# The opening part of a graph and mixture layer on one core: x normalised first, on two engines, with the edge tables behind it

## What is computed

```python
xn = _layernorm(x, axis=-1)                         # (x - mean) / sqrt(var + 1e-5)
x = x + gnn(xn, edges) + mix(xn)
x = x + ffn(_layernorm(x, axis=-1))
# gnn: msg_sum = segment_sum(xn[src], dst); mean = msg_sum / max(count, 1); two linear maps, relu, a third map
# mix: linear attention: kv = k^T v over all nodes, then q kv, gelu, w2
# ffn: a shared expert plus the best 2 of 8 experts for each row
```

## Time and profile before

| | us |
|---|---|
| median of 3 runs | 2733.04 (2730.94 to 2736.2) |
| profiled execution, own time | 2729.84 |
| its span | 2728.1 |
| its mean granted TensorE clock | 0.947 of full |
| busy PE, POOL, DVE, ACT | 2360.3, 1854.2, 1072.0, 801.6 |

### The profile page before, as it was taken

The page is one execution under the profiler, slowest core; times in us unless marked ns, Lnnn a source line. Parts: engine busy times, 40 slices in busy tenths (PEclk is TensorE's granted clock), DMA queues, the critical chain, the costliest instruction groups (busy, mean ns, idle before and its releaser), DMA issues.

```text
span 2728.1 us, 51754 instructions
## 1 busy us (share of the span) xinstructions
PE 2360.3 (87%) x12344; PEld 2030.3 (74%) x12345; DVE 1072.0 (39%) x3479; ACT 801.6 (29%) x1897; POOL 1854.2 (68%) x1790
## 2 busy tenths in 40 slices
PE   0688867877789999999999999999999999997998
PEld 0455556666678888888788888888887888876987
DVE  8545443333333343333343343433333333432221
ACT  1234312222223323232323233232323233223332
POOL 2677767777777777777777777777777777751221
PEclk9899978888899999999999999999999999998999
DMA  8333433344355555555555555555555555544764
GB/s 276 84 104 101 120 92 113 107 115 115 113 159 161 175 145 172 144 175 153 166 163 148 171 143 172 143 174 142 175 155 162 164 146 175 143 143 125 225 182 108
DMA packets 256254, 405.91 MB, mean 149 GB/s; under 512 B 70073, under 2 KB 187001, under 8 KB 255578
## 3 DMA queue, kind: packets, MB, share of 16 engines
q0 software_dynamic: 95360, 232.54, 31.9%
q1 hardware_dynamic: 154218, 164.36, 18.6%
q10 hardware_dynamic: 6384, 6.42, 0.7%
HBM read 362.16 MB, written 41.01 MB: 148 GB/s over the span
## 4 chain that ended last, share of the span: by engine, by line
PE 57%; issue 14%; POOL 13%; DVE 7%; DMA 4%; DVEq 2%; ACT 1%; ACTq 1%; POOLq 0%; SPq 0%; PEldq 0%
PE p_agg L1400 15%; POOL region L521 13%; PE p_h L1610 10%; PE p_y L1621 10%; PE p_h L1578 5%; PE p_h L1736 3%; PE p_a L1610 2%; PE p_y L1584 2%; DMA region<-xn_d,idx_s 2%; PE p_agg L1762 2%; PE p_a L1552 1%; PE p_c L1561 1%; PE p_a L1550 1%; PE p_y L1762 1%; PE p_t L1429 1%
## 5 line engine op out<-in xcount | busy, mean ns | idle before, releaser
L521 POOL DMA_INDIRECT region<-xn_d,idx_s x1568 | 1555.4, 992 | 573.3 <-issue 467.0
L1400 PE MATMUL p_agg<-region,onehot 128*128 128x258 f32 x3136 | 781.5, 403 | 123.2 <-DMA region<-xn_d,idx_s 106.4
L1400 PEld LDWEIGHTS p_agg<-region,onehot 128*128 128x128 f32 x3136 | 619.0, 201 | 234.0 <-issue 116.1
L1610 PE MATMUL p_h<-wkv_s,region 128*128 128x256 f32 x936 | 277.3, 458 | 105.8 <-ACT wkv_s L670 105.8
L1610 PEld LDWEIGHTS p_h<-wkv_s,region 128*128 128x128 f32 x936 | 210.3, 231 | 157.9 <-issue 120.7
L868 DVE TENSOR_TENSOR late<-late,p_agg 128x258 f32 x176 | 74.6, 424 | 612.3 <-PE p_agg L1400 438.4
L862 DVE TENSOR_TENSOR onehot<-row_s,iota_s 128x896 f32<-128x896 f32 (+1 forms) x225 | 246.0, 1093 | 172.4 <-issue 169.5
L1621 PE MATMUL p_y<-region 128*128 128x256 f32 x1248 | 282.3, 379 | 0.0
L691 ACT ACTIVATE work<-p_h,b1s_s 128x128 f32<-128x128 f32 x392 | 112.0, 368 | 511.6 <-PE p_h L1578 511.6
L1621 PEld LDWEIGHTS p_y<-region 128*128 128x128 f32 x1248 | 236.9, 190 | 32.5
L1584 PE MATMUL p_y<-w2s_s,work 128*128 128x256 f32 x768 | 197.3, 379 | 0.0
(11 more groups left out here) (256 smaller groups left out, 2900.3 us busy)
## 6 DMA issues: line engine op xcount, KB each, us to landing
region<-in_w1p SPq DMA_DIRECT2D x55, 1024.0 KB
region<-in_w2p SPq DMA_DIRECT2D x55, 1024.0 KB, 10.0
region<-xn_d,idx_s POOLq DMA_INDIRECT x1568
rows_s<-slot_d SPq DMA_DIRECT2D x39, 258.0 KB
region<-in_x SPq DMA_DIRECT2D x7, 896.0 KB, 5.1
xn_d<-region ACTq DMA_DIRECT2D x7, 896.0 KB, 7.0
rows<-in_x SPq DMA_DIRECT2D x49, 128.0 KB, 2.3
xnr_s<-xn_d SPq DMA_DIRECT2D x49, 128.0 KB, 2.7
```

The source lines that it names most:

```text
L521: pool.indirect_dma_start(out=ring[b][:, u, 0:D], out_offset=None, in_=xn_d, in_offset=IND(ap=idx_s[b][:, u:u + 1], axis=0)).then_inc(s_ro ...
L1400: m = mm(p_agg[b % 2], onehot[:, b % 2, u, :], ring[b][:, u, :], start=u == 0, stop=u == U - 1)
L1610: m = mm(h_wide[j], w1p_s[0][:, c, j * P:(j + 1) * P], xgt_s[:, c, :], start=c == 0, stop=c == KD - 1)
```

## The change

Four edits to the opening part:

- SP loads x first and `dst` behind the seventh chunk. The first four loads of indices stand ahead of the wait for `xnst`.
- VectorE runs the loop over the chunks first, and the work on `dst` behind it.
- In each chunk ScalarE normalises 5 of the 7 tiles (`BY_ACT = 5`), as x times scale plus bias, from rs and a new column nb = -mean times rs that VectorE writes. VectorE keeps 2 tiles. ScalarE waits for both parts before it stores the chunk.
- TensorE raises `pass_` by 4 before its waits.

```diff
+BY_ACT = 5
@@ sync
-            sp.dma_start(dst32_s, dst).then_inc(S["dstin"], 16)
             for c in range(NT // XCH):
                 if c:
                     sp.wait_ge(S["xin"], 16 * c)
                 sp.dma_start(x_s[:, c * XCH:(c + 1) * XCH, :],
...
+            sp.dma_start(dst32_s, dst).then_inc(S["dstin"], 16)
             for to, of in loads:
                 sp.dma_start(to, of).then_inc(S["wts"], 16)
 
             sp.wait_ge(S["const"], 3)
             sp.dma_start(out[NP:NP + P // 2, :], zero_s[0:P // 2, :]).then_inc(S["ost"], 16)
-            sp.wait_ge(S["xnst"], 16 * (NT // XCH))
...
             for b in range(RING):
                 load_idx(b, NI - 1)
+            sp.wait_ge(S["xnst"], 16 * (NT // XCH))
             sp.wait_ge(S["span"], 2)
@@ scalar, in the loop over the chunks
                 nc.scalar.activation(sd_s[:, 0:XCH], ve_s[:, 0:XCH], ACT.Sqrt).then_inc(S["sd"], 1)
+                act.wait_ge(S["nrm"], c + 1)
+                for j in range(BY_ACT):
+                    xj = x_s[:, ds(c * XCH + j, 1), :].squeeze(1)
+                    i = nc.scalar.activation(xj, xj, ACT.Identity, bias=nb_s[:, j:j + 1], scale=rs_s[:, j:j + 1])
+                i.then_inc(S["xna"], 1)
+                act.wait_ge(S["xna"], c + 1)
                 act.wait_ge(S["xn"], c + 1)
@@ vector
-            dve.wait_ge(S["dstin"], 16)
-            def pads_first(to):
-                V.tensor_copy(to[:, 0:2 * U], dst32_s[:, NG * U:])
-                return V.tensor_copy(to[:, 2 * U:], dst32_s[:, 0:NG * U])
-
-            own.step(pads_first(dst_s))
-            own.step(V.tensor_scalar(dst32_s, dst32_s, P - 1, None, ALU.bitwise_and))
-            own.step(pads_first(row_s))
-            own.step(V.tensor_reduce(ext_s[:, 0:NS], dst_s[:, 0:NS * U].rearrange("p (g u) -> p g u", u=U), AX, ALU.max))
-            own.step(V.tensor_reduce(ext_s[:, NS:], dst_s[:, 0:NS * U].rearrange("p (g u) -> p g u", u=U), AX, ALU.min))
-            V.tensor_scalar(ext_s[:, NS:], ext_s[:, NS:], -1.0, None, ALU.mult).then_inc(S["ext"], 1)
             with dve.Fori(0, NT // XCH) as c:
...
                 own.step(V.reciprocal(rs_s[:, 0:XCH], sd_s[:, 0:XCH]))
-                for j in range(XCH):
+                V.scalar_tensor_tensor(out=nb_s[:, :], in0=mv_s[:, :, 0:1].squeeze(2), scalar=-1.0, in1=rs_s[:, 0:XCH],
+                                       op0=ALU.mult, op1=ALU.mult).then_inc(S["nrm"], 1)
+                for j in range(BY_ACT, XCH):
                     xj = x_s[:, ds(c * XCH + j, 1), :]
                     i = V.tensor_scalar(xj, xj, mv_s[:, j, 0:1], rs_s[:, j:j + 1], ALU.subtract, ALU.mult)
                 i.then_inc(S["xn"], 1)
+            dve.wait_ge(S["dstin"], 16)
+            def pads_first(to):
+                V.tensor_copy(to[:, 0:2 * U], dst32_s[:, NG * U:])
+                return V.tensor_copy(to[:, 2 * U:], dst32_s[:, 0:NG * U])
+
+            own.step(pads_first(dst_s))
+            own.step(V.tensor_scalar(dst32_s, dst32_s, P - 1, None, ALU.bitwise_and))
+            own.step(pads_first(row_s))
+            own.step(V.tensor_reduce(ext_s[:, 0:NS], dst_s[:, 0:NS * U].rearrange("p (g u) -> p g u", u=U), AX, ALU.max))
+            own.step(V.tensor_reduce(ext_s[:, NS:], dst_s[:, 0:NS * U].rearrange("p (g u) -> p g u", u=U), AX, ALU.min))
+            V.tensor_scalar(ext_s[:, NS:], ext_s[:, NS:], -1.0, None, ALU.mult).then_inc(S["ext"], 1)
@@ tensor
+            pe.sem_inc(S["pass_"], RING)
             pe.wait_ge(S["wts"], WTS)
             pe.wait_ge(S["const"], 3)
             pe.wait_ge(S["span"], 2)
-            pe.sem_inc(S["pass_"], RING)
```

More of the change, by code:

```diff
@@ L258, in gps_layer @@
         hm_s = sb("hm_s", [P, NH2])
+        nb_s = sb("nb_s", [P, XCH])
         c_s = sb("c_s", [P, 2])
@@ L297, in gps_layer @@
         WIDE, SEVERAL = 2 ** RING, 4 ** RING
-        names = """wts const dstin xin xn xnst aggz ext extr span own_dve
+        names = """wts const dstin xin xn nrm xna xnst aggz ext extr span own_dve
             idx0 idx1 idx2 idx3 oneh pass_ added xoneh xpass
```

## The result

| | before | after |
|---|---|---|
| median of 4 runs each, us | 2731.99 (2728.66 to 2736.2) | 2691.0 (2686.12 to 2696.28) |
| ratio | | 0.985, 95% interval 0.9826 to 0.9873 |
| profiled execution, own time | 2729.84 | 2691.19 |
| its span | 2728.1 | 2689.4 |
| its mean granted clock | 0.947 | 0.956 |

The gain is 41 us, 38.7 in the profiled spans. In what follows each group of experiments was run beside the kernel before on its own chip (medians 2730.08, 2730.32 and 2731.3). The kernel after was timed on the first chip alone, so it is compared with the experiments across chips.

The account below looks back on a forecast made before the run. The first stage was taken as a gather chain begun by the first gather, which DMA traffic limits. Its 11.25 us lead less 1.0 for company gave -10.2: from 2733.04 to 2722.8 us, 8-in-10 range 2716 to 2729.

Parts of the forecast that it names:

- the first gather: GpSimd's first gather in the opening: start at 64.5 us instead of 75.75, 11.25 earlier, with DMA traffic as the limit.
- in well before: Opening's DMA traffic: the last store, issued at 50.7 us, lands well before the weights at 63.4.
- The loads of x: Opening: loads with a store beside them take about 6.7 us, so the last x load is issued at 37.0.
- The row of 6.7: Earlier trace's row for an x load with a store beside it: 6.7 us, against 5.1 alone.
- the rival with the cast of the earlier trace: Opening: chunk 0 stands until GpSimd's clearing ends at 14.66 us; costs 2.1 us, total 2724.9; chance 0.10.
- one of the signs named for a wrong prediction: Opening: a VectorE instruction of the first chunk lasting until 14.7 us would show the prediction wrong.
- the two-scalar rows: Earlier trace: two-scalar `tensor_scalar` takes 410 ns, median 412 beside gathers; so chunk 0 was taken as unhindered by GpSimd.
- the first single-source instruction of the loop: Loop over x on VectorE: by the shared-port rule, this instruction would stand until GpSimd's clearing ends at 14.66 us.
- the loop and what lies behind it: Opening: ScalarE sets 5.7 us a chunk; reduction ends at 57.5, tables run 63.6 to 74.3, first sums at 80.9.
- the company: First gathers now run beside VectorE's tables: a cost of 1.0 us, between 0 and 3.
- The rival in which they hold each other: Tables and gathers delay each other in L805 to L851: tables end at 101.7, total 2742.5 us; chance 0.04.
- What the first gather gains, the end gains too: Whole run: the first gather's lead, 11.25 us, carries to the end if the rest keeps pace.

Follow-up runs that it names:

- 4 fillers: Kernel after plus four VectorE instructions that only raise an unused semaphore, ahead of the tables: 2715.7 us, ratio to before 0.9946.
- 252: Kernel before plus 252 VectorE raises of an unused semaphore ahead of the tables: 2727.8 us in one execution.
- 4 at the end: Kernel after plus four VectorE raises of an unused semaphore behind all of VectorE's loops: 2688.05 us, ratio to before 0.9858.
- 2 fillers: Kernel after plus two VectorE raises of an unused semaphore ahead of the tables: 2699.05 us in one execution.
- 64, 128 and 192: Kernel after plus that many VectorE raises of an unused semaphore ahead of the tables: 2687.04, 2690.84 (one execution) and 2694.17 us.
- the split alone: Kernel before with ScalarE normalising 5 of 7 tiles per chunk, VectorE 2; load order, dst work and first `pass_` raise unchanged: 2702.31 us, ratio 0.9898.

## Why the prediction was right, and where it was wrong

*Right, the first gather.* 64.5 was forecast, 64.39 measured. The weights landed at 62.9 (63.4), the traffic of 36 to 62 us was 383 GB/s (364). The indices bound it, and with these moved, the last store: the queues are the limit. That it fitted to 0.1 us is luck in part: 9.0 MB had moved by 37 us and not 9.2, and the rest then went at 380 GB/s and not 364. The last store, held to be "in well before" the weights, landed at 63.26, behind them. Two more terms erred and did no harm. The loads of x were not held by the stores: 5.2 us each, last issue at 32.6 and not 37.0. The row of 6.7 was a single one; now the stores were slow, 9.5 us in the median (7.0 before). And the first chunk did stand until 14.69, as the rival with the cast of the earlier trace rows had it; it was one of the signs named for a wrong prediction. I had read the two-scalar rows as speaking against it, but what stood was the small `ve_s` instruction ahead of them. The fourteen instructions of the statistics before it (6.08 to 9.15 us) were not held, so "the first single-source instruction of the loop" was too wide. The Trainium skill's rule of the exclusive lock ("SBUF — State Buffer", "SBUF: two separate sides") agrees with the row. The rival's price, 2.1 us, did not show; the loads ran ahead meanwhile, which I take for the reason, but no run tests it.

*Right, the loop and what lies behind it.* Pitch 5.5 us (forecast 5.7), five activations 2.56 (3.0), the dst part from 49.12 to the reduction at 56.37 (55.7 to 57.5 for raise and end of it), the tables 62.94 to 74.2 (63.6 to 74.3), the first sums at 80.08 (80.9).

*Nearly right, the company.* The first six pitches of the gathers took 7.77 us (64.39 to 72.16 in the timeline) against 7.56 undisturbed: 0.2 and not 1.0. The tables took 11.3 us. The rival in which they hold each other does not occur.

*Right, the gain of the opening.* The kernel with the new opening and the late code at its old place leads by 12.1 us at tile 11 and by 14.4 in the median (interval 10 to 19 from its ratio); -10.2 was the sum. At tile 11 the difference to the sum is 1.9 us: the first gather came at 64.0 and not 64.5 there, and the company cost 0.2 and not 1.0; 0.6 I can't place. Behind tile 11 lie two more short iterations than before (3.4 us) and ScalarE's 0.05 us in each.

*Wrong: "What the first gather gains, the end gains too", and the sum made of that alone.* Each edit was priced where it stands. The sum had no term for what it does to code that isn't edited: five instructions out and one in shift every later instruction of VectorE. That term is 24.7 us by the run with 4 fillers, 2.4 times the rest of the sum, and it was put at nothing without a reason. It is made of 0.40 us in each of 48 iterations, on the chain that TensorE waits for, and of a clock that stays at full more often when that wait is shorter. The first part is shown by the gap, by its return with 4 fillers, its absence with 252 and with 4 at the end; that a load of code is behind it is inferred from this and from where the packets lie. The second is a count: of 36 iterations, kernels with the gap had 4 to 6 short ones, those without it 10 to 14. It holds for the untraced executions too: in all that enter the ratios here, the mean granted clock was 0.945 to 0.953 in all kernels with the gap, and 0.951 to 0.957 in all without it; 2 fillers, between the two, gave 9 and 0.949. Why one wait of 2.31 us is followed by the lower clock and another isn't, no run here shows.

Could it have been forecast? That later code would move was in the diff. The gap of 0.61 us, 48 times, at an addition whose operands had long been there, was in the trace of before. That four places would be enough to cover it could not be read, only tried. A chance and a range of both signs for it would have been right.

## What to carry to other kernels

- When a diff changes the number of an engine's instructions ahead of a long loop, look whether the loop has changed too (2 and 4 fillers changed it, 64, 128 and 192 did not). Look for a gap on that engine in which it waits only for itself and longer than between like pairs (0.61 us against 0.21 here); if TensorE waits for that chain, multiply by the iterations.
- To compare two versions of anything, bring the loop to the same place with instructions that do nothing, or the comparison measures the place: the split alone "gained" 27.8 us, and all but some 2 us of that was the place.
- In an opening whose queues are full, count the bytes: 18.85 MB at the rate that the trace of before shows gave the first gather within 0.2 us, and moving the indices further forward in that queue gave nothing.

## What the hardware showed that I had not expected

- In each iteration of this loop 8192 bytes of VectorE's code are loaded 5 times, and at one of these places VectorE stood 0.40 us; the place repeats with 128 instructions (none and 128 more), 4 fewer and 252 more give the same 0.21 us, and a shift of 2 leaves 0.15 bare.
- With the loop 64 or 192 instructions further on nothing of it is loaded again (30 packets in place of 268), and it is no faster for that.
- A change to ScalarE's opening part took 0.05 us off a pause of ScalarE in every late iteration.
- 0.44 us less of waiting per iteration of 44 gave 7 more iterations (11 of 36 instead of 4) at full clock, 1.7 us each: almost as much again as the wait itself.
- Seven clears of 1806 columns back to back keep VectorE's 7-column instruction out as long as one of 12642 (5.53 and 5.50 us).
- Five activations of 256 columns with scale and bias per partition take 2.56 us, 0.51 each, though one with bias alone takes 0.46 and begins alone.
